# Expert weights of a routed feed-forward layer, loaded in four parts of 320 KB instead of one of 1280 KB

## The reference

```
x = norm(x + decayed_linear_attention(x))        # 16 heads, chunks of 128
x = norm(x + int8_feed_forward(x))               # 512 -> 2048 -> 512
x = norm(x + q * cumsum(k * v) * sigmoid(g))     # four 512 x 512 products with bias
x = norm(x + routed_experts(x))
```

```
g, u = split(x @ wgu[e].T, 2)                    # 512 -> 192 and 192
y   += (silu(g) * u) @ wd[e].T * cw[:, None]     # 192 -> 512
```

## Time and profile before

| | |
|---|---|
| time, median of 3 runs | 1674.09 us (1671.94 to 1676.6) |
| profiled execution, its time | 1671.12 us |
| profiled execution, span from first to last instruction | 1668.7 us |
| mean granted TensorE clock | 0.954 of full |

### The profile page before, as it was taken

One profiled execution on the slowest core, in us unless ns is written; L12 is line 12 of the kernel. 1 busy time (PEld: TensorE's weight loads), 2 busy tenths in 40 slices (PEclk: granted clock), 3 DMA queues, 4 the chain that ended last, 5 costly groups with the idle time before them and its releaser, 6 DMA issues.

```text
span 1668.7 us, 33852 instructions
## 1 busy us (share of the span) xinstructions
PE 1475.8 (88%) x11445; PEld 837.1 (50%) x11446; DVE 966.5 (58%) x1883; ACT 716.3 (43%) x1295; POOL 777.0 (47%) x683
## 2 busy tenths in 40 slices
PE   4799999999999999999995469889888999999980
PEld 2466666644444444455553236546545665656640
DVE  6777777786757666634888754334333444443437
ACT  5344334466464645434555334334333444444430
POOL 2465445550010102133565255565555876766654
PEclk9899999999999999999997579999999999999995
DMA  6132211169777767421111058899998987877878
GB/s 230 52 109 62 83 25 25 27 227 320 234 261 230 262 222 262 168 77 51 53 53 53 1 188 229 239 248 259 278 254 233 168 157 139 145 144 140 146 101 306
DMA packets 97101, 269.51 MB, mean 162 GB/s; under 512 B 15152, under 2 KB 15568, under 8 KB 91920
## 3 DMA queue, kind: packets, MB, share of 16 engines
q1 hardware_dynamic: 61424, 182.75, 32.9%
q0 software_dynamic: 35616, 85.99, 26.2%
HBM read 158.84 MB, written 101.47 MB: 156 GB/s over the span
## 4 chain that ended last, share of the span: by engine, by line
PE 63%; DVE 14%; DMA 12%; issue 4%; ACT 3%; POOL 2%; DVEq 0%; SPq 0%; ACTq 0%; POOLq 0%
PE bank L532 15%; PE bank L848 14%; DMA acc<-X,WA 10%; PE bank L869 7%; PE bank L660 6%; PE bank L666 6%; PE bank L689 6%; PE bank L839 3%; DVE ARENA L1039 2%; ACT ARENA L1329 1%; DMA ARENA<-acc 1%; PE bank L858 1%; PE bank L769 1%; DVE ARENA L1217 1%; PE bank L521 1%
## 5 line engine op out<-in xcount | busy, mean ns | idle before, releaser
L848 PE MATMUL bank<-ARENA,XT 128*128 x1908 | 366.3, 329 | 1.6 <-DVE XT L1291 1.4
L1735 POOL DMA_INDIRECT acc<-X,WA x159 | 252.9, 1590 | 183.6 <-ACT X L1329 138.9
L848 PEld LDWEIGHTS bank<-ARENA,XT 128*128 128x128 f16 x1908 | 181.4, 99 | 124.5 <-issue 8.8
L869 PE MATMUL bank<-ARENA,XT 128*128 x795 | 199.1, 381 | 25.6 <-issue 14.0
L1291 DVE COPY XT<-bank 128x1024 f16<-128x1024 f16 x159 | 109.9, 691 | 185.4 <-PE bank L839 184.8
L1329 ACT ACTIVATE ARENA<-ARENA 128x512 f16<-128x512 f32 (+1 forms) x128 | 93.9, 736 | 256.5 <-DVE ARENA L1067 133.4
L1729 POOL DMA_INDIRECT XT<-x_rows,WA x159 | 157.5, 991 | 56.8 <-issue 36.6
L532 PE MATMUL bank<-WA,XT 128*128 128x512 f16 (+1 forms) x768 | 136.7, 332 | 22.8 <-DVE WA L908 19.6
L1591 POOL TENSOR_TENSOR rstd<-mv,mhalf 128x1 f32<-128x1 f32 x44 | 19.1, 435 | 287.9 <-DVE mv L914 287.9
L532 PE MATMUL bank<-XT,STG 128*128 128x512 f16 x640 | 149.9, 381 | 0.0
L1301 DVE SCALAR_TENSOR_TENSOR XT<-bank,XT 128x192 f32<-128x192 f32 x159 | 66.4, 418 | 140.5 <-ACT XT L1568 131.0
(11 more groups left out here) (218 smaller groups left out, 2399.9 us busy)
## 6 DMA issues: line engine op xcount, KB each, us to landing
w_scratch<-WA SPq DMA_DIRECT2D x64, 640.0 KB, 3.9
ARENA<-w_scratch SPq DMA_DIRECT2D x32, 1280.0 KB
ARENA<-w_exp SPq DMA_DIRECT2D x48, 640.0 KB, 5.3
WA<-w_exp SPq DMA_DIRECT2D x16, 640.0 KB, 5.1
ARENA<-ARENA SPq DMA_DIRECT2D x64, 128.0 KB, 2.3
acc<-ARENA SPq DMA_DIRECT2D x18, 256.0 KB, 3.0
x_rows<-ARENA SPq DMA_DIRECT2D x17, 256.0 KB, 2.3
STG<-xT SPq DMA_DIRECT2D x8, 512.0 KB, 4.8
```

Of the source, the lines that this page charges most:

```text
L848: mm = pe.matmul(d, xTb[k.u % 2][:, a * KD + kd, :], weights(sl, b, kd * 2 * DFF, 2 * DFF), start=(a, b, kd) == (0, 0, 0), stop=(a, b, kd) ...
L869: mm = pe.matmul(d, hT[k.u % 2][:, c, :], weights(sl, j, c0, DIM), start=n == 0, stop=n == 4)
L1735: pool.indirect_dma_start(acc[i % 2], bass.IndirectOffsetOnAxis(blkidx[:, i:i + 1], 0), yD[i % 4], None, compute_op=ALU.add).then_inc(y_ou ...
```

## The change

Each expert's load is cut by columns into four parts of 2560 bytes per partition (320 KB). SyncE issues a part, waits until it has landed, and issues the next. The semaphore now rises by 64 per expert in place of 16, and TensorE waits for all four parts of its expert.

```diff
             def load_expert(e):
                 sl = e % NSLOT
-                sp.dma_start(Wslot[:, sl * 2 * WCOLS:(sl + 1) * 2 * WCOLS], wsp[e].rearrange("p j n -> p (j n)")).then_inc(w_in, 16)
-                sp.wait_ge(w_in, 16 * (e + 1))
+                rows = wsp[e].rearrange("p j n -> p (j n)")
+                for c in range(4):
+                    part = slice(c * WCOLS // 2, (c + 1) * WCOLS // 2)
+                    sp.dma_start(Wslot[:, sl * 2 * WCOLS:(sl + 1) * 2 * WCOLS][:, part], rows[:, part]).then_inc(w_in, 16)
+                    sp.wait_ge(w_in, 16 * (4 * e + c + 1))
...
                 sl = e % NSLOT
-                pe.wait_ge(w_in, e * 16 + 16)
+                pe.wait_ge(w_in, e * 64 + 64)
                 pe.wait_ge(xt_sb, k.i + 1)
```

## The result

The changed kernel takes 1816.71 us (median, 1813.46 to 1818.8), against 1673.01 us of the kernel before on the same chip: ratio 1.0869, 95% interval [1.0845, 1.0894]. The forecast was 1753 us; the loss is 144 us where 80 were forecast. The profiled execution took 1817.46 us with a span of 1814.5 us.

The account below looks back on a forecast made before the run. Scatters were taken to bound the kernel, the loader after the change: 28 loads of 13.5 us (10.8 + 0.6 + 2.15) end at 1384.1 us, plus 364.4 us tail, 2.4 and 3.0 us: forecast 1753 us, range 1704 to 1821.

Parts of the forecast that it names:

- What bounds it: Expert loop while weights load: scatters set the pace, 4.20 us per block against 3.79 later; the loading chain is nearly full.
- Part 1: Weight loads: each part in series pays its own path, 2.7 us a part, 10.8 us for four against 6.0 before.
- the store of 256 KB: Lower bound for a weight part: such a store lands after 2.3 us, plus 0.1 us to the next issue, 2.4 us.
- Part 2: SyncE's reading and checking of the release count, once per expert and not per part: 0.6 us per expert.
- Part 3: Weight loads beside gathers and scatters: the four parts together lose what one load loses now, 2.15 us per expert.
- Part 4: Expert loop: first four loads hidden, then the loader at 13.5 us against TensorE's 9.0 us per expert; +80 us.
- (a): Rival, expert loop: small packets let scatters through, blocks take 3.79 us, -29 us, 1645 us; chance of faster 0.05.
- break-even: Loader in the expert loop: 10.65 us per expert, (1304.3 - 1006.1) / 28; below it the change wins something.
- (b): Rival, TensorE's clock: it stays at half level for whole experts after weight waits, 53 us more, 1806 us; chance 0.08.
- (c): Rival, weight loads: each part loses what a load loses now, 20 us per expert, 1935 us; chance 0.07 above 1821.

Follow-up runs that it names:

- no_traffic: The changed kernel without its scatters and with only the first 8 gathers, whose rows serve all blocks: 1710.21 us (one execution).
- first_four_at_once: The changed kernel with the parts of experts 0 to 3 issued together, the rest in series: 1812.67 us, ratio 1.0844.
- by_rows: The changed kernel with its four parts in series cut by partitions (32 partitions with 10,240 bytes each): 1843.6 us, ratio 1.1043.
- four_at_once: The changed kernel with an expert's four parts issued back to back and one wait for all: 1657.08 us, ratio 0.9915 against the kernel before.

## Why the prediction was right, and where its size was off

**What bounds it.** Right, and so are the direction and the mechanism; the size was too small, 80 us for 144. The loss ends with the last weight load, the tail kept its length, and the loader replaced the scatters as the pace-setter. It never waited for a slot.

The time measured lies 4 us inside the upper end of the range, 1821 us. That end stood for parts of 3.1 us and 2.9 us of contention, with load 4 at 1006 us. What was measured is a cheaper part, more contention and a later load 4; that the last landing of that end (1451 us) meets the 1450.4 us of the trace is partly luck.

**Part 1, a part in the quiet.** Forecast 2.7 us, 10.8 us for four; `no_traffic` shows 2.88 us and 11.5 us. 0.7 us too little, 20 us over 28 experts. The upper bound (all 2.15 us of a load's path are paid per part, 3.1 us) was nearer than the store of 256 KB.

**Part 2, SyncE's own work.** Forecast 0.6 us; 12.1 - 11.5 leaves 0.6 us.

**Part 3, contention.** This is the term that was mis-sized most: 2.15 us per expert forecast. From the issue of load 4 at 1017.2 us on, an expert takes (1450.4 - 1017.2) / 28 = 15.5 us, less 12.1 alone 3.4 us (3.3 by the waits): 1.2 us too little, 34 us. Two things were left out. The 2.15 us was taken as a loss on the packets, shared out by bytes, but each part's path is met by traffic too: the packet records of the trace give 1.6 us of packets and 1.4 us of path for a part in the quiet, 2.1 and 1.75 us beside traffic (mean of the four parts, both with SyncE's work once in four). And the fourth part loses 1.60 us and the others 0.58: by the same records a fourth part meets 6.0 packets of gathers and scatters per engine, a second part 0.6. TensorE starts again when a fourth part has landed, and the traffic of its blocks falls on the same parts of the cycle each time; that this is the reason is argued from the records and was not tried by itself.

**Part 4, what is hidden.** That the first four loads are hidden, so that load 4 goes out at 1006 us, was wrong: it went out at 1017.2 us, 11 us later. Loads 0 and 1 took 12.3 and 11.9 us in place of 10.8, nearly in the quiet, and loads 2 and 3, which met the first gathers and scatters, 15.6 and 17.0 us. `first_four_at_once` takes the late start away and is only some 4 us faster, within the noise. TensorE waits for a gated load from expert 4 on (1037.4 us), not from the ninth or tenth. The count of waits (25 against some 22) and their length (5.2 against 4.5 us) fit.

20 + 34 + 11 = 65 us; the distance from the forecast's 1384.1 us for the last landing to 1450.4 is 66 us, the rest is rounding.

**Rivals.** (a) Relief is real and does not show: scatters land in 5.3 us, yet an expert's parts took 12.1 us with no traffic at all, above the 10.65 us of break-even. (b) The clock did fall, and by the waits it was free; that this rival's 1806 us lie nearer to the time measured than the forecast does is luck. In order of time around one long wait, TensorE in the changed kernel:

```profile
1349.10 1.46 PE L851 MATMUL bank<-ARENA,XT 128*128 x8
...
1361.22 2.74 PE L851 MATMUL bank<-ARENA,XT 128*128 x8 [8.32 <-DMA ARENA<-w_scratch]
1363.75 1.06 PE L842 MATMUL bank<-ident,XT 128*128 128x128 f16 x8
```

The granted clock of the stretches in which they lie (last column but two):

```profile
1349.10:1353.00 3.90, 3.80 (x29) 2.18 (x27) 1.54 (x4) 1.82 (x6) 2.52 (x2) 1.00 0.71 202
1361.20:1363.70 2.50, 2.48 (x8) 1.26 (x9) 0.00 (x0) 0.00 (x0) 0.00 (x0) 0.50 0.49 124
```

Eight products take 1.46 us at a granted clock of 1.00, the 2.4 GHz level, and 2.74 us after a wait of 8.3 us at 0.50, the 1.2 GHz level. The Trainium skill ("TensorE: Matmul & The Clock Gate", section "Why this matters for your kernels") says that idle gaps between bursts do this; the trace agrees. Against the earlier trace rows the stretch has a granted clock of 0.87 in place of 0.98, and TensorE is busy 301.62 us for nearly the same matmuls, 34 us more:

```profile
1007.00:1450.00 443.00, 301.62 (x1992) 178.92 (x1990) 110.02 (x287) 114.81 (x287) 183.69 (x143) 0.87 0.74 172
1450.00:1750.00 300.00, 290.60 (x2220) 181.44 (x2221) 121.49 (x316) 125.24 (x316) 201.48 (x157) 1.00 0.79 142
```

All of it lies inside the time that the next weights took anyway: SyncE never waited for a block to be done. (c) Contention by a part's packets would cost 8.6 us per expert; the change shows 3.4 us. The bytes alone would leave 2.15 us, so the truth lies between the two, and `by_rows` does not tell which of them it follows.

The Trainium skill's rule of 1 MiB per DMA ("DMA: Bandwidth & Descriptors", "Rules for kernel authors") pointed the right way for parts in series. For parts on their way together the kernel was faster with 320 KB each than with 1280 KB, but not because the load was: counted from its first issue, its last packet ended after 8.3 us in `four_at_once` and after 7.6 us in the kernel before, on average.

## What to carry to other kernels

A wait after each part makes every part pay its whole path: 2.9 us for 320 KB here, of which 1.6 us are packets, and before splitting one should compare parts x that price with the time in which the consumer wants the next piece (12.1 us against 9.0 us here). The price grows where other queues are busy, here by 0.6 us on each of the first three parts and 1.6 us on the fourth, on average, and it is paid on the path as well as on the packets. If a load is to be cut at all, issue all parts at once and wait once: four parts gave 0.9% here, two gave 0.3%, and eight made the weights late.

## What had not been expected

- A load cut by partitions (32 partitions of 10,240 bytes per DMA) is slower than one cut by columns: 1843.6 against 1816.7 us in series, 1699.5 against 1657.1 us together, with scatters landing after 8.2 us against 7.1 us. Alone, a part of it takes 3.3 us where one cut by columns takes 2.9 us.
- Four DMAs on their way together, with the same bytes as one, made the kernel before faster (ratio 0.9915), though its weights were never late.
